# Last layer's edges: one-hots read their keys as three rows of 256 with a gap, and are split 8 and 17 over the halves of a turn

## What is computed

```python
msgs = z[edge_dst] @ Wd + z[edge_src] @ Ws + edge_weight[:, None] * ww[None, :] + bm
agg = jax.ops.segment_max(msgs, edge_dst, num_segments=n)
agg = jnp.where(deg[:, None] > 0, agg, jnp.zeros((), dtype=z.dtype))
hidden = jax.nn.relu(z @ W1a + agg @ W1b + b1)
return hidden @ W2 + b2
```

## Time and profile before

| | us |
|---|---|
| median of 3 runs | 4696.24 |
| lowest and highest of them | 4684.4 and 4727.59 |
| the profiled execution's own time | 4732.81 |
| its span in the trace | 4731.1 |
| last layer's edges in it (first scan's memset to the end of the last second half) | about 3810 to 4662 |

### The profile page before, as it was taken

How to read it: one execution, slowest core, us unless ns; L and a number is a source line. 1 busy time by engine, 2 the same in 40 slices (tenths; PEclk the granted TensorE clock), 3 DMA queues, 4 the chain that set the end, 5 groups by cost and what they waited for, 6 DMA issues and landing times. The chain is left out here.

```text
span 4731.1 us, 59027 instructions
## 1 busy us (share of the span) xinstructions
PE 2085.7 (44%) x11198; PEld 1170.4 (25%) x11198; DVE 3503.5 (74%) x6910; ACT 2759.8 (58%) x6194; POOL 3349.4 (71%) x2987
## 2 busy tenths in 40 slices
PE   1879999999861000000002200000000659888895
PEld 1434545454430000000001100000000335555553
DVE  5545555555464999999997588888888567777776
ACT  0868888888535888888882332222222345555553
POOL 5688888888717777777753677777776267777774
PEclk7989999999985555555556655555555779999997
DMA  9965555555543777777774466666665233333332
GB/s 322 348 156 98 102 102 100 99 103 103 117 108 118 280 277 284 273 287 270 287 267 151 157 219 210 213 220 211 210 220 184 63 102 119 117 115 116 109 118 84
DMA packets 298355, 832.36 MB, mean 176 GB/s; under 512 B 64549, under 2 KB 190261, under 8 KB 288898
## 3 DMA queue, kind: packets, MB, share of 16 engines
q1 hardware_dynamic: 116796, 565.99, 32.0%
q0 software_dynamic: 172208, 260.10, 24.5%
q10 hardware_dynamic: 9238, 5.24, 0.4%
HBM read 378.43 MB, written 452.66 MB: 176 GB/s over the span
## 5 line engine op out<-in xcount | busy, mean ns | idle before, releaser
L686 POOL DMA_INDIRECT tab<-arena x560 | 944.7, 1687 | 208.7 <-issue 141.9
L827 PE MATMUL psum<-arena 128*128 128x512 bf16 (+1 forms) x4704 | 950.2, 357 | 0.0
L1653 PE MATMUL psum<-ident,arena 128*128 128x128 f32 x15 | 3.7, 426 | 2119.6 <-DVEq L1681 2119.6
L2026 POOL DMA_INDIRECT arena<-table,arena x784 | 748.6, 955 | 242.5 <-issue 238.5
L2526 POOL DMA_INDIRECT arena<-table,arena x622 | 648.6, 1043 | 192.7 <-issue 181.5
L2608 PE MATMUL psum<-arena 128*128 (+1 forms) x4050 | 698.0, 336 | 102.1 <-DVE arena L2656 61.1
L1402 POOL DMA_INDIRECT arena<-table,arena x588 | 578.4, 984 | 179.2 <-issue 176.1
L827 PEld LDWEIGHTS psum<-arena 128*128 128x128 bf16 x4704 | 434.0, 99 | 474.2 <-issue 25.3
L1653 PEld LDWEIGHTS psum<-ident,arena 128*128 128x128 f32 x15 | 2.7, 212 | 2120.2 <-DVEq L1681 2119.9
L2608 PEld LDWEIGHTS psum<-arena 128*128 (+1 forms) x4050 | 406.1, 100 | 386.4 <-issue 137.9
L1464 ACT ACTIVATE arena<-arena 128x128 f32<-128x128 f32 x1344 | 402.0, 387 | 59.4 <-issue 39.9
(11 more groups left out here) (424 smaller groups left out, 5085.9 us busy)
## 6 DMA issues: line engine op xcount, KB each, us to landing
rows<-arena SPq DMA_DIRECT2D x56, 3808.0 KB
arena<-seg_rows SPq DMA_DIRECT2D x112, 896.0 KB, 6.8
rows<-arena SPq DMA_DIRECT2D x56, 1008.0 KB, 4.7
rows<-arena SPq DMA_DIRECT2D x56, 896.0 KB
seg_rows<-arena SPq DMA_DIRECT2D x40, 896.0 KB
arena<-table,arena POOLq DMA_INDIRECT x1994
arena<-src_lanes SPq DMA_DIRECT2D x56, 448.0 KB
seg_rows<-arena SPq DMA_DIRECT2D x8, 1792.0 KB
```

The lines of the kernel that those rows point to most:

```text
L686: eng.indirect_dma_start(out=m.tabs[j], out_offset=bass.IndirectOffsetOnAxis(ap=idx[g][:, k:k + 1], axis=0), in_=rows[g][:, k, 0:D], in_of ...
L827: t = eng.matmul(ps[:, c, 0:w], part[n // 2 % PAIRS][:, n % 2, :], hot[n % HOTS][:, lo:lo + w], start=False, stop=False, skip_group_check= ...
L2026: eng.indirect_dma_start(out=kv[k][:, j, :], out_offset=None, in_=m.table2, in_offset=bass.IndirectOffsetOnAxis(ap=idx[k][:, j:j + 1], axi ...
```

## The change

The tile of keys gets three rows of 258 float16, of which 256 are used, so that two elements lie idle between rows. The DMA that loads the keys writes the three rows, and the comparison reads them so. Its output is the same 768 adjacent elements, only named in three pieces of 256. `EARLY` goes from 13 to 8: of the 25 one-hots of a turn 8 are now made in the first half and 17 in the second. Lines below the first hunk lie 3 further down.

```diff
+KEY_ROWS, KEY_ROW = 3, BATCH // 3
...
-        keys = A(BATCH, dt=F16)
+        keys = A(KEY_ROWS, KEY_ROW + 2, dt=F16)[:, :, 0:KEY_ROW]
...
-                    eng.dma_start(keys, m.src_lanes[t, :].rearrange("t l -> (t l)").partition_broadcast(P)).then_inc(keys_in, 16)
+                    eng.dma_start(keys, m.src_lanes[t, :].rearrange("(a t) l -> a (t l)", a=KEY_ROWS).partition_broadcast(P)).then_inc(keys_in, 16)
...
-                    eng.tensor_scalar(hot[b], keys, block_ids[:, b:b + 1], None, ALU.is_equal).then_inc(hot_made, 1)
+                    eng.tensor_scalar(hot[b].rearrange("p (a k) -> p a k", a=KEY_ROWS), keys, block_ids[:, b:b + 1], None, ALU.is_equal).then_inc(hot_made, 1)
...
-                EARLY = HALF - 1
+                EARLY = 8
```

## The result

The changed kernel takes 4780.8 us (median, 4777.76 to 4800.21) against 4693.7 for the kernel before: 1.0185 times as long, with a 95% interval of 1.0153 to 1.0218. The forecast was 4738 us, which would have been no difference that can be told; the change is slower by 1.85%, and the time lies 7 us inside the upper end of the range, 4688 to 4788. One more execution of the kernel before is in its median now, which was 4696.2. The profiled execution took 4783.0 us, its span is 4781.3.

The account below looks back on a forecast made before the run. POOL's gathers were taken to bound the stage before, a TensorE-ScalarE-VectorE ring after: 6 + 26 x (30.9 - 29.86) = 33 us, plus 9 us towards the median, on 4696.2 gives 4738 us; range 4688 to 4788.

Parts of the forecast that it names:

- Part 1, the form: Keys in three rows: a one-hot on VectorE goes from 0.335 to 0.55 us and may stop holding up POOL's gathers.
- Costs nothing by itself: VectorE's 5.4 us more a turn for slower one-hots fits, barely, into its 8 to 9 us free.
- The load of the keys: DMA writing 384 pieces of 256, not 128 of 768: put at nothing, at worst eating about 3 us of room.
- Part 2, the ring: With 8 and 17, TensorE, ScalarE and VectorE wait on each other in a closed chain: 29.6 us a turn, clock up.
- The clock: TensorE's clock drops after idling 3.2 us before block 7: 1.3 us more a turn, making it 30.9.
- The sum against the profiled execution: Turn 1 6 us later plus 26 longer turns: 33 us over the profiled 4732.8, giving 4766 us.
- From the profiled execution to the median: 9 us added for part of the 36.6 us by which the median lies below the profiled execution.
- The clock that stays up: Rival: TensorE's clock does not fall, turns of 29.6 us, 4705 us; chance 0.12.
- POOL's pace: Rival: TensorE's chain of waits doesn't bind, POOL's gathers set 27.5 us a turn, about 4640 to 4650 us; chance 0.10.
- the held POOL: Rival: one-hots still hold up POOL's gathers, 5.3 us when caught, turns of 32.2 us, 4763 us; chance 0.08.
- L520's pace: Rival: one-hots slow to 0.94 us, VectorE bounds at 36.9 us a turn, 4886 us; chance 0.04.
- The clock costs as after longer idle times: Rival: TensorE's clock loss is 2.4 us a turn, turns of 32.0 us, 4766 us; chance 0.12.

Follow-up runs that it names:

- e1: Changed kernel with EARLY back at 13 (keys still in three rows); 4709.2 us against 4723.1 for the kernel before, ratio 0.9969.
- e9: Changed kernel with ScalarE copying the next indices, then scaling the second half, then evicting; 4687.9 us against 4696.3 for the kernel before, ratio 0.9978.
- e4: Changed kernel with 24 unread matmuls between TensorE's blocks 6 and 7; 4745.6 us against 4723.1 for the kernel before, ratio 1.0073.
- e2: Kernel before with EARLY = 8 alone, keys still in one run of 768; 4785.2 us against 4723.1, ratio 1.0149.
- e6: Changed kernel with EARLY = 10 (10 and 15 one-hots); 4704.7 us against 4711.9 for the kernel before, ratio 0.9971.
- e7: Kernel before, unchanged, run and profiled a second time; 4714.0 us, ratio to itself 1.0001.
- e3: Kernel of e1 with keys in two rows of 384 instead of three; 4726.0 us against 4723.1 for the kernel before, ratio 1.0031.
- e8: Changed kernel, run and profiled again; 4803.3 us, ratio 1.0171 to the kernel before.
- e5: Changed kernel with ScalarE scaling the second half ahead of eviction and next indices; 4800.8 us against 4711.9 for the kernel before, ratio 1.0198.

## Why the prediction was right in kind, and too small in size

It had the mechanism, the direction of its likeliest number and a range that holds the result. Its number is 43 us low, so that it took the loss for too small to tell. That the range holds 4780.8 is in part luck: its upper end came from a longer clock penalty and from gathers still held, and what was missing lay mostly in another term.

- **Part 1, the form.** Right in direction and size. A one-hot of 0.55 us was forecast and 0.524 measured (the estimate by the Trainium skill had given 0.535). In the turns POOL is held nowhere. Over the whole stage the sign "no gather over 1.1 us" failed once: in turn 0, beside VectorE's splitting of the table, a gather of 3841.90 takes 5.39 us, and the kernel before has one of 5.49 at the same place. "Costs nothing by itself" is shown by e1. The load of the keys, put at nothing, is waited for 8.9 us; the load issued at 4216.62 let the one-hot go at 4220.10, 3.5 us later, 0.3 us later than VectorE was ready. Within the room that was named, here; in e9, with the ring open, it is 37.9 us.
- **Part 2, the ring.** Right. 29.6 us forecast, 29.75 measured where the clock is held up (e4). 11.9 us from TensorE's last block to its next group forecast, 11.87 measured. POOL waits 4.4 us a turn (110.7 / 25), where some 3 were forecast. Idle 3.2 us forecast, 3.13 to 3.18 measured. e2 shows it without the form, e6 shows its edge, e9 opens it.
- **The clock.** This term was too small: 1.3 us a turn, measured 1.8 to 2.0 (31.56 - 29.75, or 19.7 us in the mean for 18 blocks less 17.7). The ten turns it was taken from had idle times of 2.25 to 2.94 us and the new one is 3.13, and two of the ten had no loss; here no turn is without. Over 26 turns it is about 17 us (26 x (31.56 - 30.9)).
- **The sum against the profiled execution.** 33 us forecast, 50 measured; the 17 between them are the clock.
- **From the profiled execution to the median.** This step fell furthest short: 9 us were put on, and the medians differ by 87.1 where the profiled executions differ by 50.2, so 37 were needed. The profile of before stood 36.6 us above its median. In its stage 17 gathers were held by a batch of one-hots; e7 has 7 and a stage 22 us shorter, and e3, whose one-hots take as long as before, has 4 and one of 819.8 us (31 us shorter). The first profile had caught gathers more often than these two did, and the ring has no such luck. So the stage accounts for 22 to 31 of the 37 us, if these profiles are like most executions, which three profiles can't show. What starts before the stage varies too: it began between 3802 and 3839 us in twelve profiles of unchanged code. Why is not known. With 30 in place of 9 the forecast would have been 4759, slower by 1.3%, and with the clock's 17 us as well 4776.
- **Rivals.** The clock that stays up, POOL's pace, the held POOL and L520's pace are all excluded by the profile after. "The clock costs as after longer idle times" (4766) came nearest, with 2.4 us a turn for 1.9. Two slips of the pen in them change nothing: the clock that stays up adds up to 4702 and not 4705 (4696.2 - 3 + 9), and L520's pace is taken as 1.04 ns an element in one place and 1.06 in another, where its row gives 1.07.

## What to carry to other kernels

When work is moved from one part of a loop to another, write down for each consumer which item of it is the first to be made late, what that item waits for in the order of every engine, and follow that back until it meets itself; if it does, the length of the ring is the time of a turn, whatever the busy shares say. An engine's order is part of such a ring: in this one, three calls on ScalarE written in another order are worth 1.9% (1.0171 in e8, 0.9978 in e9), and the first attempt at them (e5) only closed a second ring. And where a profile's own time stands off the median, look first whether the stage under study is one that varies; a change that makes it steady is measured against its usual length and not against the profiled one.

## What the runs showed of the hardware

- A gather on GpSimd's queue was held by a batch of the old one-hots only if it began 0.17 to 0.36 us behind the batch. All 28 that were held (17 in the kernel before, 7 in e7, 4 in e3) began so, behind the batch of 11 in a second half, and took 3.45 to 3.62 us; 14 others that began in the same window behind such batches passed in 1.00 to 1.20. So the window is needed and isn't enough. In the earlier trace rows the gather of 4211.68 began 0.19 us after the batch of 4211.49 and took 3.61; one already under way when the batch of 4200.21 began (4200.10, 0.94 us) was let through, and so was the next, at 1.05 us. In e2 gathers passed through 16 one-hots in 1.02 us each. The Trainium skill (page SBUF — State Buffer, section Who interferes with whom) has the one that comes second block fully; here it did so in a narrow window of beginnings, and not always there. What decides it was not tried.
- TensorE's clock fell behind the stops of 3.13 to 3.18 us in all 26 turns of the changed kernel, which costs 1.8 to 2.0 us a turn, and behind those of 2.8 us in e2, which costs 1.5. The length of the stop alone doesn't decide it: in turn 1 of e9 TensorE stopped for 3.70 us, and blocks 7 to 24 took 17.87 us with the clock at 1.00 (the row below). In e4 24 matmuls that nobody needs gave back 47 us of 821.

```profile
3855.04 17.87 PE L2611 MATMUL psum<-arena 128*128 x108 [3.70 <-DVE arena L2659]
```

- With its input in three rows and its output in one run a comparison of 768 float16 takes 0.524 us in a batch and 603 ns by itself; with one row or two, 0.335 and 411 to 412.
